# Every whole tile of source rows gathered by GpSimd, none by SyncE or ScalarE row by row

## What is computed

```python
h = maximum(layernorm(x), 0)                       # layer 0: attention
p = h @ W + b_lin                                  # 4 heads of 32
logits = leaky_relu(sum(concat(p[src], p[dst]).reshape(-1, H, 2*C) * alpha, -1), 0.2)
att = exp(logits - segment_max(logits, dst)[dst]); att /= segment_sum(att, dst)[dst]
x = x + segment_sum(att * p[src], dst) + bias
h = maximum(layernorm(x), 0)                       # layer 1: edge features
ef = (relu(edge_attr @ We1 + be1) @ We2 + be2) * sigmoid(ts @ Wt + bt)
msg = relu(concat(h[src], ef) @ Wn1 + bn1) @ Wn2 + bn2
x = x + segment_sum(msg, dst) + h
```

## Time and profile before

| | |
|---|---|
| median of 3 runs | 3255.13 us (3254.9 to 3264.79) |
| the profiled execution | 3247.73 us, its span 3245.9 us |
| TensorE busy (weight loads) | 1748.3 us, 54% (1199.9 us, 37%) |
| VectorE busy | 1541.0 us, 47% |
| ScalarE busy | 604.1 us, 19% |
| GpSimd busy | 1554.8 us, 48% |
| DMA | 213.29 MB, mean 66 GB/s |

### The profile page before, as it was taken

One profiled execution on the slowest core, in us unless ns is written; L12 is line 12 of the kernel. 1 busy time (PEld: TensorE's weight loads), 2 busy tenths in 40 slices (PEclk: granted clock), 3 DMA queues, 4 the chain that ended last, 5 costly groups with the idle time before them and its releaser, 6 DMA issues.

```text
span 3245.9 us, 44492 instructions
## 1 busy us (share of the span) xinstructions
PE 1748.3 (54%) x8785; PEld 1199.9 (37%) x8785; DVE 1541.0 (47%) x5471; ACT 604.1 (19%) x1276; POOL 1554.8 (48%) x1650
## 2 busy tenths in 40 slices
PE   2245443443433344253536775666666666766668
PEld 2233332332322233232334443444444444444446
DVE  2255545454433444354554554444444444444447
ACT  2320000000000000000235332222222222222223
POOL 5515555554544545453063554544445455444451
PEclk9665555555555555555667887877777788777788
DMA  4201111111111111111032333323323333333323
GB/s 119 60 16 42 42 43 40 44 40 36 40 33 33 43 31 43 35 38 29 2 110 75 85 98 94 95 77 92 93 77 95 93 83 92 93 94 95 83 86 110
DMA packets 114385, 213.29 MB, mean 66 GB/s; under 512 B 36899, under 2 KB 78030, under 8 KB 104127
## 3 DMA queue, kind: packets, MB, share of 16 engines
q0 software_dynamic: 51424, 106.19, 13.3%
q1 hardware_dynamic: 54930, 101.96, 10.9%
q10 hardware_dynamic: 7756, 2.31, 0.4%
HBM read 197.43 MB, written 12.88 MB: 65 GB/s over the span
## 4 chain that ended last, share of the span: by engine, by line
SPq 56%; issue 34%; PE 3%; another core or an unknown queue 2%; DVE 2%; ACT 1%; DMA 0%; POOL 0%; ACTq 0%; DVEq 0%; POOLq 0%
SPq L419 24%; SPq L1320 22%; SPq L109 8%; SPq L1316 1%; SPq L1315 1%; PE pair L1424 0%; PE pair L1418 0%; DVE acc L670 0%; PE bank L1433 0%; PE bank L1444 0%; ACT feat L1475 0%; PE bank L1453 0%; DVE moments L1547 0%; ACT ef L1475 0%
## 5 line engine op out<-in xcount | busy, mean ns | idle before, releaser
L1367 POOL DMA_INDIRECT acc<-table,index x806 | 766.0, 950 | 756.8 <-DVE pre L1612 461.5
L472 POOL DMA_INDIRECT rows<-table,index x753 | 716.4, 951 | 737.1 <-PE pair L973 386.0
L1418 PE MATMUL pair<-ea,we 64*128 64x512 f32 x416 | 271.6, 737 | 305.4 <-DMA ea<-in_ea_t 295.7
L665 DVE TENSOR_SCALAR onehot<-iota_row,dst_rel 128x128 f32<-128x128 f32 x808 | 238.4, 296 | 373.3 <-remote 310.2
L1627 DVE TENSOR_TENSOR acc<-acc,bank 128x128 f32 x832 | 239.0, 287 | 300.1 <-remote 122.6
L973 PE MATMUL pair<-onehot,rows 128*128 128x128 f32 x1560 | 380.7, 418 | 0.0
L973 PEld LDWEIGHTS pair<-onehot,rows 128*128 128x128 f32 x1560 | 327.6, 309 | 64.0 <-issue 59.0
L670 DVE TENSOR_TENSOR acc<-acc,pair 128x256 f32 x832 | 349.0, 420 | 4.3 <-issue 1.3
L1433 PEld LDWEIGHTS bank<-wn1b,ef 128*128 128x128 f32 x1664 | 273.8, 236 | 165.1 <-issue 116.5
L1424 PE MATMUL pair<-hidden,we 128*128 128x512 f32 x416 | 281.1, 763 | 78.3 <-ACT hidden L1503 68.2
L1593 DVE SCALAR_TENSOR_TENSOR ef<-pair,be,gate 128x512 f32<-128x512 f32 x208 | 155.3, 746 | 331.1 <-PE pair L1424 234.8
(11 more groups left out here) (186 smaller groups left out, 1539.2 us busy)
## 6 DMA issues: line engine op xcount, KB each, us to landing
ts<-in_ts SPq DMA_DIRECT2D x52, 1024.0 KB
rows_x<-table SPq DMA_DIRECT2D x2176, 0.5 KB
rows_y<-table SPq DMA_DIRECT2D x2048, 0.5 KB
ea<-in_ea_t SPq DMA_DIRECT2D x52, 512.0 KB
moments<-table ACTq DMA_DIRECT2D x1536, 0.5 KB
rows_z<-table ACTq DMA_DIRECT2D x1024, 0.5 KB
acc<-table,index POOLq DMA_INDIRECT x806
rows<-table,index POOLq DMA_INDIRECT x753
```

Of the source, the lines that this page charges most:

```text
L472: gp.indirect_dma_start(rows0[:, n % (RING * TG), :], None, table1, bass.IndirectOffsetOnAxis(index[:, n:n + 1], 0)).then_inc(half_in[g % ...
L1367: gp.indirect_dma_start(rows[:, g % RG1, t, :], None, table, bass.IndirectOffsetOnAxis(index[:, n:n + 1], 0)).then_inc(gathered[g % RG1], 16)
L1418: pe.matmul(bank[g % 2][:, :], we1[:, :], ea[:, g // HALF % 2, edges(g)], start=True, stop=True).then_inc(h1, 1)
```

## The change

The four lists of tiles that SyncE and ScalarE fetch are emptied. As all else is worked out from these lists, GpSimd gathers the 830 whole tiles of both layers (it gathered 801 and 806), SyncE fetches the ten rows of the short tile in each layer, and ScalarE none. In layer 1 SyncE's loop over `LINE_TILES1` has no passes, so that its loads of `ea` and `ts` all stand in the loop behind it, one after the other.

```diff
-LINE_TILES = [g * TG for g in (21, 29, 37, 53, 61, 77, 85, 101, 109, 117, 133, 141, 157, 165, 181, 189, 197)]
+LINE_TILES = []
 LINE_STEP = 12
-LINE_TILES1 = [g * TG for g in range(LINE_STEP + 7, GROUPS, LINE_STEP)]
+LINE_TILES1 = []
...
-ACT_TILES0 = [SPANS[r][0] * TG + 1 for r in range(ACT_TURNS + 2, TURNS, ACT_TURNS)]
+ACT_TILES0 = []
...
-ACT_TILES = [g * TG for g in range(ACT_STEP + 2, GROUPS, ACT_STEP)]
+ACT_TILES = []
```

## The result

| | before | after | ratio, 95% interval |
|---|---|---|---|
| median of 4 runs each | 3255.02 us (3248.12 to 3264.79) | 2843.56 us (2837.22 to 2853.64) | 0.874 (0.870 to 0.877) |
| the profiled execution | 3247.73 us, span 3245.9 us | 2840.72 us, span 2838.9 us | |
| a second chip, 7 and 4 runs | 3326.00 us (3312.64 to 3330.13) | 2854.92 us (2830.38 to 2858.83) | 0.857 (0.852 to 0.861) |
| a third chip, 7 and 4 runs | 2133.92 us (2130.47 to 2136.96) | 2172.21 us (2168.66 to 2174.82) | 1.018 (1.016 to 1.020) |

The third line is the surprise of this case: on another chip the same change costs 1.8%. Everything down to the experiments is about the first chip, to which the prediction was made.

The account below looks back on a forecast made before the run. One-row fetches by SyncE and ScalarE were taken as the bound, with held reports next. Savings of 204 us in layer 0 and 181 in layer 1 made 385; 3247.7 less that is 2863, plus 7 is 2870 us, range 2800 to 2990.

Parts of the forecast that it names:

- the held reports: Both layers: while GpSimd issues gathers, what TensorE finishes is seen late, mostly at GpSimd's next pause; 310.2 us before L665.
- Layer 0, 204 us: Layer 0 saving: 235.7 us idle before L625 gone, 35 us of gathers added, 3 us small gains; bounds 90 to 236.
- three runs of eight: Layer 0 span: three GpSimd runs of 11.9 us each, some 14.5 for a fourth with the turn, about 50 us.
- 115 us extra in all: Layer 0: a report held back at GpSimd's fourth run would cost about 5 us a span.
- Layer 1, 181 us: Layer 1 saving: last gather starts at 3004 instead of 3184.49, with 97 cycles and six more gathers.
- the cycle: Layer 1: eight gathers and a pause take 12.6 us, 6.3 us a group; bounds 12.4 to 13.3.
- A: Rival, both layers: fetched rows hold the reports, not GpSimd, so GpSimd's own pace decides; 2390 us, chance 0.06.
- `ea` hidden: Layer 1: the load of `ea`, gated by its buffer alone, is issued some 25 us ahead and lands in 6 us.
- Gathers stretch (D): Rival: gathers lengthen beside denser vector work, 0.085 us each for some 1510 gathers, 128 us; 2998 us, chance 0.07.
- Shorter runs (B): Rival: GpSimd gathers four at a time, 7.7 us a group in layer 1, 277 us more; 3147 us, chance 0.15.
- long runs (C): Rival, layer 1: reports held through long runs, 121 us per twelve groups instead of 76; 3610 us, slower, chance 0.04.
- The price of 35 us for 28 more gathers in layer 0: Layer 0: 28 added gathers lie on the path at 1.25 us each; bounds 0 to 60 us.

Follow-up runs that it names:

- light_sync: Kernel after with 12 tiles of layer 0 and 10 of layer 1 given back to SyncE, on a holding chip: 2969.63 us, 0.893 of the kernel before.

## Why the prediction was right, and where it was not

The forecast was 2870 us, within 2800 to 2990; 2843.56 was measured. The sum was made for the profiled run, 2863, and that took 2840.72: 22 us too high.

**What bounds it.** Right: the chain lost SPq (56% to 0%), idle time before L625 and L1418 went to 0.0, and the held reports stayed as the next thing. Why a fetched row took 0.70 us was not asked; no run on a free chip shows so much (0.41 us there, see above).

**Layer 0, 204 us.** 203.0 were measured, and yet the form is another. A span takes 49.7 us in the mean (50 was said, 56.7 it was). I had three runs of eight at 11.9 us and 14.5 for the rest; most spans have two runs of twelve, and a held report now lies in the turn of the span (760.79, 7.69 us), which I had priced at 115 us extra in all. Longer runs have fewer pauses, which I take to have paid for it; the two were not measured apart. That they nearly cancel is luck: the 204 is right in size and only partly in mechanism.

**Layer 1, 181 us.** Measured 200: from the first gather that waits for the ring (1569) to the last (2778.2) 1209 us, and 1409 before; I had 1228. The mis-sized term is the cycle, 12.6 us per eight gathers taken from the earlier trace rows; it is 1209 / 97.75 = 12.37, as runs of twelve take 18.6 us, 12.4 per eight. It lies just below the bounds that I gave (12.4 to 13.3). I had said that a shorter cycle speaks for A, but here it comes from longer runs, with the waits for "remote" still there. The last 4 us lie between the layers (0.6), in the filling of layer 1's ring (2.7) and in the tail (0.7), which the sum took as unchanged.

**`ea` hidden.** Right: L1418 has no idle time. **Gathers stretch (D).** No: the median is 944 ns as before, the largest 1056 and 1166. The free chip, with VectorE 70% busy (54% on the first), has the same median. So no run shows the median gather lengthened by more work of VectorE. The upper part of D needed 0.26 us more for each gather, and the means are 947 and 950 ns, where they were 950 and 951. A mask of VectorE lasts 0.29 us, so that waiting one out would, as an estimate from that, lengthen a gather by no more; 59 of the 1612 gathers do last over 1 us. **Shorter runs (B), long runs (C).** Neither: runs grew from eight gathers to twelve, and the pause before a run in layer 1 only from 2.85 or 2.92 us to 3.9. **A.** With ten fetched rows in each layer the reports are held as long as before, so the fetches aren't needed for that. That they don't add to it is not shown: light_sync speaks for some effect of theirs, or of the pattern.

**The price of 35 us for 28 more gathers in layer 0** can't be read from the result, and light_sync shows that the sum must not be run in reverse: 22 tiles fewer for GpSimd were 115 us slower and not 28 faster. Where runs and spans lock into a pattern, a term per tile gives the mean only.

**What the prediction could not hold.** It took the held reports, and the 0.70 us of a fetched row, for properties of the program. They go with the chip: the kernel after has 282 waits for "remote" on one chip and none on another, and four variants of it have none on a third. (Each chip was used at one time only, so that something else that changed with it is not ruled out.) On the one free chip where it was run several times, the change makes the time longer by 1.8%. The pace is the one I had priced for rival A (1.25 us a gather in layer 1, 40 us a span; measured 1.25 and, from the ninth span on, 40.5), but the kernel before was at 2134 us already, as fetched rows are cheap on such a chip (0.41 us), and I had not asked what one more gather costs once GpSimd is the bound.

## What to carry to other kernels

An engine that the chain calls idle may be idle only because its neighbours are held up (in the kernel after GpSimd is idle for 533.6 us before L1367 on the holding chip and for 258.8 on a free one): before work is moved to it, work out its own floor (gathers x 1.25 us, here 1612 x 1.25 = 2015 us; on the free chip they took 2032 of 2170 us) and compare it with the time that is hoped for. If a profile has waits for which it finds no source on the core, ask for a run on another chip before the split of the work is tuned, since here the same change saved 13% on one kind and cost 1.8% on the other. The price of an operation can go with what another engine does at that moment (here a fetched row, 0.40 us while GpSimd was idle and 0.80 us while it gathered, in one place of one trace of a holding chip): measure it in both conditions. Where work came in runs locked against a second cycle, a cost per piece measured in one pattern didn't carry to another (22 tiles moved from GpSimd to SyncE were 115 us slower, not 28 faster).

## What the runs showed of the hardware

Two kinds of behaviour for one program. The spans of the kernel after, 2838.9 us on a holding chip and 2169.7 on a free one, differ by 669 us: 34 before the first gather of the table (96.7 and 63.1), 256 while layer 0 gathers (1247.6 and 991.9), 60 between the layers (119.1 and 58.9), 275 while layer 1 gathers (1314.8 and 1040.0) and 45 behind the last (60.7 and 15.8). Neither do the gathers differ (944 ns in the median on both) nor does how long VectorE works (1536.6 and 1525.2 us), but the waits with no source on this core do, 282 of them with 1267 us in all on the holding chip and none on the free one. TensorE differs too: it is busy 1705.1 us at a granted clock of 0.698 on the holding chip, and 1562.7 us at 0.783 on the free one. Whether the lower clock follows from the waits no run tells; its 142 us more of work are in any case far less than the 669. The last 45 us are no held report of that moment, as no wait for "remote" stands behind the last gather: on the holding chip GpSimd runs ahead of the sums, so that more groups are still to be summed behind the last gather (12 of the adds of L1612 start behind it, and 2 on the free chip). Why a chip holds TensorE's reports while GpSimd issues gathers stays open; with two gathers at a time and a pause behind them (1.30 and 2.24 us in the rows shown) it didn't, from 1700 to 2300 us. SyncE's fetched rows show the same two kinds: 0.75 to 0.78 us each beside the gathers of a holding chip, 0.41 beside those of a free one.
